# A four-layer gated cross-attention decoder: GpSimd's constants in pieces between its first stores, and two buffers of squares in the key preparation

## The reference, cut to what matters

```python
x = x + jnp.tanh(g_xattn[0]) * _L0_xattn_ref(_layernorm(x, axis=-1), ctx_1024, ctx_1024, L0_xattn_Wq, ...)
x = x + jnp.tanh(g_ffn[0]) * _L0_ffn_ref(_layernorm(x, axis=-1), ...)
...
x = x + jnp.tanh(g_xattn[2]) * _L2_xattn_ref(ctx_1024, _layernorm(x, axis=-1), L2_xattn_Wq, ...)
...
x = x + jnp.tanh(g_xattn[3]) * _L3_xattn_ref(ctx_1024, ctx_1024, _layernorm(x, axis=-1), mask_Bx1xS2_bf1, ...)
x = x + jnp.tanh(g_ffn[3]) * _L3_ffn_ref(_layernorm(x, axis=-1), ...)
```

```python
qh = (q @ Wq + bq).reshape(B, Lq, H, D).transpose(0, 2, 1, 3)
kh = (k @ Wk + bk).reshape(B, k.shape[1], H, D).transpose(0, 2, 1, 3)
vh = (v @ Wv + bv).reshape(B, v.shape[1], H, D).transpose(0, 2, 1, 3)
att = jnp.einsum('bhqd,bhkd->bhqk', qh, kh) * scale
att = jax.nn.softmax(att, axis=-1)
y = jnp.einsum('bhqk,bhkd->bhqd', att, vh)
```

## Time and profile before

| | |
|---|---|
| median of 3 runs | 3102.66 us (3099.45 to 3102.67) |
| the profiled execution's own time | 3106.83 us |
| its span in the profile | 3105.2 us |
| mean granted TensorE clock | 0.984 of full speed |
| busy: PE, ACT, DVE, POOL | 97%, 81%, 15%, 7% of the span |
| context preparation, first scores at | 118.06 us from the span's start |

### The profile page before, as it was taken

One profiled execution on the slowest core, in us unless ns is written; L12 is line 12 of the kernel. 1 busy time (PEld: TensorE's weight loads), 2 busy tenths in 40 slices (PEclk: granted clock), 3 DMA queues, 4 the chain that ended last, 5 costly groups with the idle time before them and its releaser, 6 DMA issues.

```text
span 3105.2 us, 54465 instructions
## 1 busy us (share of the span) xinstructions
PE 3003.0 (97%) x18636; PEld 1135.6 (37%) x18636; DVE 465.9 (15%) x1308; ACT 2520.9 (81%) x2893; POOL 205.7 (7%) x732
## 2 busy tenths in 40 slices
PE   5899999999999799999999998999899999999999
PEld 3333333323333433333333334666522222322257
DVE  2310010100011400111101004544200000100012
ACT  2699999999943399999999996322399999999963
POOL 3000000000000000000000002000000000000000
PEclk8999999999999899999999999999899999999999
DMA  5222122111230112122211124010011111111110
GB/s 156 74 65 72 49 68 72 37 37 57 62 86 1 25 56 63 55 68 65 65 38 39 58 61 120 30 38 1 5 38 37 37 37 50 51 38 37 37 38 7
DMA packets 167027, 157.25 MB, mean 51 GB/s; under 512 B 20872, under 2 KB 121724, under 8 KB 166844
## 3 DMA queue, kind: packets, MB, share of 16 engines
q1 hardware_dynamic: 159872, 149.27, 16.1%
q0 software_dynamic: 1088, 3.34, 0.3%
q10 hardware_dynamic: 5884, 2.08, 0.3%
HBM read 121.89 MB, written 32.91 MB: 50 GB/s over the span
## 4 chain that ended last, share of the span: by engine, by line
PE 93%; DVE 4%; issue 1%; ACT 1%; POOL 1%; DMA 0%; SPq 0%; ACTq 0%; DVEq 0%; POOLq 0%
PE PS L2299 40%; PE PS L2318 31%; PE PS L768 5%; PE PS L753 5%; PE PS L755 2%; PE PS L1108 2%; PE PS L1098 1%; PE PS L1566 1%; PE PS L1563 1%; PE PS L1142 0%; PE PS L1099 0%; PE PS L2279 0%; PE PS L2212 0%; PE PS L2285 0%; PE PS L1128 0%
## 5 line engine op out<-in xcount | busy, mean ns | idle before, releaser
L2074 ACT ACTIVATE probs<-PS 128x1024 f32<-128x1024 f32 x2496 | 2283.3, 1228 | 41.3 <-PE PS L2318 36.3
L2299 PE MATMUL PS<-probs,vr 128*32 128x512 f32 (+1 forms) x9984 | 1326.7, 604 | 1.9 <-DVE accs L2544 1.9
L2318 PE MATMUL PS<-qs,kr 35*128 35x512 f32 (+2 forms) x4992 | 1066.0, 482 | 8.1 <-issue 3.1
L2318 PEld LDWEIGHTS PS<-qs,kr 35*128 35x128 f32 x4992 | 448.8, 184 | 1183.3 <-ACT probs L2074 816.9
L791 ACT ACTIVATE probs<-PS 128x512 f32<-128x512 f32 x192 | 114.5, 598 | 272.8 <-PE PS L753 144.7
L1905 POOL COPY vr<-vs 128x72 f32 (+1 forms) x624 | 157.8, 253 | 2672.6 <-PE PS L2299 2474.5
L2299 PEld LDWEIGHTS PS<-probs,vr 128*32 128x32 f32 x9984 | 197.3, 108 | 339.7 <-issue 273.4
L768 PEld LDWEIGHTS PS<-wide,probs 128*128 128x128 f32 x1280 | 151.5, 194 | 17.5 <-issue 16.7
L768 PE MATMUL PS<-wide,probs 128*128 128x128 f32 x1280 | 153.8, 277 | 0.5 <-DVE kf L826 0.5
L2544 DVE COPY accs<-PS 128x512 f32<-128x512 f32 x12 | 8.3, 692 | 749.4 <-PE PS L2285 749.4
L753 PE MATMUL PS<-xT,wide 128*128 128x512 f32 x224 | 106.7, 594 | 1.0 <-DVE probs L810 1.0
(11 more groups left out here) (312 smaller groups left out, 1169.4 us busy)
## 6 DMA issues: line engine op xcount, KB each, us to landing
kr<-key_pieces SPq DMA_DIRECT2D x1248, 64.0 KB
key_pieces<-kparts SPq DMA_DIRECT2D x172, 96.0 KB, 2.8
kr<-mask_strips SPq DMA_DIRECT2D x624, 4.0 KB
values<-kf SPq DMA_DIRECT2D x34, 216.0 KB, 4.1
vs<-values SPq DMA_DIRECT2D x2, 3672.0 KB, 16.7
c_T<-turned_context SPq DMA_DIRECT2D x18, 192.0 KB, 4.0
key_pieces<-probs SPq DMA_DIRECT2D x32, 96.0 KB, 3.0
c_in<-turned_context SPq DMA_DIRECT2D x16, 192.0 KB, 4.1
```

The source lines that it names most:

```text
L2074: sc.activation(prob[n % RING][:, :, q0:], PS[:, bank:bank + 2, q0:], ACT.Exp, scale=SCALE).then_inc(p_ready, 1)
L2299: last = te.matmul(PS[32 * j:32 * j + 32, 7, q0:], vr[s.buf(c)][:, at_v:at_v + 32], prob[(n + j // 2) % RING][:, j % 2, q0:], start=fresh, ...
L2318: last = te.matmul(o, kr[b][own, p, :], qs[own, T8 // 2 * s.hh + p, 512 * s.qh + q0:512 * s.qh + 512], start=True, stop=True)
```

## The change

Three edits, all in the first 100 us of the program.

- **GpSimd's constants in pieces.** `const_ready` is signalled three times: behind `c_last`, which is now right behind `head_of`; behind a piece that holds what the mask and the last rows need; and behind the last constant. The other constants follow in pieces, each behind one of the first nine stores of `c_T`, whose loop is written out. ACT's wait behind step 0 is for the first signal. DVE's mask work comes behind step 2 and waits for the second. ACT (step 9), DVE (step 13) and PE (behind the preparation) wait for the third.
- **The chain with two buffers of squares.** The high part has a semaphore of its own, `k_high`; SP's first stores and DVE's low part wait for it. ACT's squares read the stored high part in SBUF instead of the keys in PSUM, into `ksq[:, b]`, and stand behind the copy of the next step. Their wait for the norms is one for two steps back, and so is PE's wait for the low part.
- **Small ones.** DVE's steps 3 to 12 are written out instead of looped. ACT issues the attention weights in steps 1 to 3 and the mask strips in step 4.

```diff
@@ gpsimd
             last.then_inc(first_const, 1)
-            g.memset(vs[:, :, :, HD:VC].rearrange("p c h o -> p (c h) o"), 1.0)
             g.memset(mask_u8[:, :], 0)
             chain(g.memset(c_last[:, :], 0.0))
-            g.memset(c_last[0:LAST, D:D + 1], 1.0)
-            pool.wait_ge(ident_ready, 1)
-            chain(g.tensor_copy(ident_b[:, :], ident[:, :]))
...
-            g.memset(run_max[:, :, :], 0.0).then_inc(const_ready, 1)
...
+            g.memset(c_last[0:LAST, D:D + 1], 1.0).then_inc(const_ready, 1)
+
+            def k_step(i):
+
+                pool.wait_ge(ct_ready, i + 1)
+                g.dma_start(ct_scr[i:i + 1, :, :].rearrange("o p k -> p (o k)"), c_T[i % 2]).then_inc(ct_out[i % 2], 16)
+
+            def row_constants():
+                g.memset(vs[:, :, :, HD:VC].rearrange("p c h o -> p (c h) o"), 1.0)
...
+            def mask_constants():
...
+                g.tensor_copy(ident_b[:, :], ident[:, :]).then_inc(const_ready, 1)
...
+            k_step(0)
+            row_constants()
+            k_step(1)
+            mask_constants()
+            k_step(2)
+            stair_constants()
+            k_step(3)
+            left_constants()
+            k_step(4)
+            pick_constants()
+            k_step(5)
+            chain(g.memset(leaf_sel[:, :, :], 0.0))
+            leaf_rows_pool(g, chain, (0,))
+            k_step(6)
+            leaf_rows_pool(g, chain, (1, 2))
+            k_step(7)
+            counts_pool(g, chain)
+            k_step(8)
+            mean_constants()
+            for i in range(9, NTILE):
+                k_step(i)
@@ sync
-                for c, done in enumerate((k_act, k_low)):
+                for c, done in enumerate((k_high, k_low)):
@@ scalar
-                if not first:
-                    act.wait_ge(kn_ps, at(j, off, 1, 0))
                 keys = PS[:, 1 + b, 0:TW]
-                sc.activation(kparts2[b][:, 0, :, 0, :], keys.rearrange("p (c k) -> p c k", c=TC), ACT.Identity, bias=bqk[:, 1, 0:1])
-                sc.activation(ksq[:, 0, :], keys, ACT.Square, bias=bqk[:, 1, 0:1]).then_inc(k_act, 1)
+                sc.activation(kparts2[b][:, 0, :, 0, :], keys.rearrange("p (c k) -> p c k", c=TC), ACT.Identity, bias=bqk[:, 1, 0:1]).then_inc(k_high, 1)
                 if not last:
                     rows(j, off + 1, first)
+                if not first:
+                    act.wait_ge(kn_ps, at(j, off, 1, -1))
+                act.wait_ge(k_high, at(j, off, 1, 1))
+                sc.activation(ksq[:, b, :].rearrange("p (c k) -> p c k", c=TC), kparts2[b][:, 0, :, 0, :].bitcast(F32), ACT.Square).then_inc(k_act, 1)
...
-                if i == 1:
+                if 1 <= i < 4:
+                    attention_weights(i - 1)
+                if i == 4:
                     strips()
-                if 2 <= i < 5:
-                    attention_weights(i - 2)
...
                 if i == 9:
+                    act.wait_ge(const_ready, 3)
                     router_weights(act)
@@ tensor
-                te.matmul(PS[0:32, 7, 0:TW], head_of[:, :], ksq[:, 0, :], start=True, stop=True).then_inc(kn_ps, 1)
+                te.matmul(PS[0:32, 7, 0:TW], head_of[:, :], ksq[:, off % 2, :], start=True, stop=True).then_inc(kn_ps, 1)
...
-                    pe.wait_ge(k_low, at(j, off, 1, 0))
+                    pe.wait_ge(k_low, at(j, off, 1, -1))
...
+            pe.wait_ge(const_ready, 3)
@@ vector
-                dve.wait_ge(k_act, at(j, off, 1, 1))
+                dve.wait_ge(k_high, at(j, off, 1, 1))
...
-            dve.wait_ge(const_ready, 1)
+            k_step(None, 1)
+            k_step(None, 2)
+            dve.wait_ge(const_ready, 2)
...
-            with dve.Fori(0, ROUNDS) as j:
-                for off in range(1, UNROLL + 1):
-                    k_step(j, off)
+            for i in range(3, TAIL[0]):
+                k_step(None, i)
             for k, i in enumerate(TAIL):
                 if k == 0:
                     dve.wait_ge(x_in, 16)
+                    dve.wait_ge(const_ready, 3)
```

More of the change, by code:

```diff
@@ L679, in flamingo_decoder, with leaf_rows_pool @@
         E1_IN = (16 * 9, 16 * 10)
-        def const_pool(g, chain):
-            chain(g.memset(leaf_sel[:, :, :], 0.0))
-            for n in range(3):
+        def leaf_rows_pool(g, chain, nets):
+            for n in nets:
                 ls = leaf_sel[:, :, :].rearrange("p c (l h) -> p c l h", l=2)
@@ L686, in const_pool, with counts_pool @@
                                       base=-32 * n, pattern=[[-2, HC], [-1, 2], [0, 64]], channel_multiplier=1))
+        def counts_pool(g, chain):
             chain(g.iota(countdown[:, :], pattern=[[-1, LEAVES]], base=LEAVES, channel_multiplier=0,
@@ L1840, in _ @@
             last.then_inc(first_const, 1)
-            g.memset(vs[:, :, :, HD:VC].rearrange("p c h o -> p (c h) o"), 1.0)
             g.memset(mask_u8[:, :], 0)
             chain(g.memset(c_last[:, :], 0.0))
-            g.memset(c_last[0:LAST, D:D + 1], 1.0)
-            pool.wait_ge(ident_ready, 1)
-            chain(g.tensor_copy(ident_b[:, :], ident[:, :]))
-            chain(g.memset(stair[:, :], 0.0))
-            chain(g.affine_select(out=stair[:, :], in_=stair[:, :], compare_op=ALU.is_ge, fill=-BIG,
-                                  base=0, pattern=[[1, P]], channel_multiplier=-1))
@@ L1850, in _ @@
[L1850 to L1878, removed]
@@ L1879, in _ @@
-            chain(g.affine_select(out=kvm, in_=kvm, compare_op=ALU.is_ge, fill=0.0,
-                                  base=HD - 1, pattern=[[HD, H], [0, HD]], channel_multiplier=-1))
-            g.memset(run_max[:, :, :], 0.0).then_inc(const_ready, 1)
[L1883 to L1888, removed]
@@ L1889, in _ @@
-            with pool.Fori(0, ROUNDS) as j:
-                for off in range(1, UNROLL + 1):
-                    k_step(j, off)
-            for i in TAIL:
-                k_step(None, i)
+            g.memset(c_last[0:LAST, D:D + 1], 1.0).then_inc(const_ready, 1)
[4 more added lines that the diff above has]
+                g.memset(vs[:, :, :, HD:VC].rearrange("p c h o -> p (c h) o"), 1.0)
+                g.memset(zero_one[:, 0, :], 0.0)
+                g.memset(zero_one[:, 1, :], 1.0)
+                chain(g.memset(valid[:, :], 1.0))
+                chain(g.affine_select(out=valid[:, :], in_=valid[:, :], compare_op=ALU.is_ge, fill=0.0,
+                                      base=CTX - 1, pattern=[[-1, P]], channel_multiplier=-P))
@@ new lines, in mask_constants, with stair_constants @@
+            def mask_constants():
+                g.memset(rows_w[:, :], 0.0)
+                g.memset(leaf_b2[:, :, :], 0.0)
+                g.memset(ones_row[:, :], 1.0)
+                chain(g.memset(valid_last[:, :], 0.0))
+                chain(g.memset(valid_last[0:LAST, :], 1.0))
+                pool.wait_ge(ident_ready, 1)
+                g.tensor_copy(ident_b[:, :], ident[:, :]).then_inc(const_ready, 1)
+            def stair_constants():
+                chain(g.memset(stair[:, :], 0.0))
+                chain(g.affine_select(out=stair[:, :], in_=stair[:, :], compare_op=ALU.is_ge, fill=-BIG,
+                                      base=0, pattern=[[1, P]], channel_multiplier=-1))
+                chain(g.memset(upper[:, :], 0.0))
+                chain(g.affine_select(out=upper[:, :], in_=upper[:, :], compare_op=ALU.is_ge, fill=-BIG,
+                                      base=0, pattern=[[-1, P]], channel_multiplier=1))
@@ new lines, in left_constants, with pick_constants @@
+            def left_constants():
+                for b in range(TC):
+                    g.memset(vr[b][:, :], 0.0)
+                g.memset(k_left[:, :].bitcast(F32), 0.0)
+                g.memset(v_left[:, :, :], 0.0)
+            def pick_constants():
+                g.memset(one_row[:, :], 0.0)
+                chain(g.memset(pick[:, :, :, :].bitcast(F32), 0.0))
+                for e in range(2):
+                    chain(g.memset(one_row[HALF * e + PROD:HALF * e + PROD + 1, :], 1.0))
+                for c in range(PARTS):
+                    for r in range(PARTS):
+                        at_r = PIECES * c + HD * r
+                        dst = pick[:, c].rearrange("p t (e x) -> p t e x", e=2)[:, :, :, at_r:at_r + HD]
+                        g.tensor_copy(dst, ident[:, :].rearrange("p (e d t) -> p t e d", e=2, d=HD))
@@ new lines, in mean_constants @@
+            def mean_constants():
+                chain(g.memset(kv_mask[:, :], 1.0))
+                kvm = kv_mask[:, :].rearrange("p (h d) -> p h d", h=H)
+                chain(g.affine_select(out=kvm, in_=kvm, compare_op=ALU.is_ge, fill=0.0,
+                                      base=0, pattern=[[-HD, H], [0, HD]], channel_multiplier=1))
+                chain(g.affine_select(out=kvm, in_=kvm, compare_op=ALU.is_ge, fill=0.0,
+                                      base=HD - 1, pattern=[[HD, H], [0, HD]], channel_multiplier=-1))
```

(1 more changed line is left out.)

5 lines of the change are left out of this document (1 added, 4 removed).

## The result

The changed kernel takes 3084.71 us (median of 5 runs, 3078.82 to 3087.39), the kernel before 3102.66 us (5 runs, 3099.45 to 3103.02). The ratio is 0.9942, 95% interval 0.9931 to 0.9954: faster by 18 us, 0.6%. The forecast was 3081 us, range 3072 to 3090. The profiled execution took 3084.71 us, its span is 3082.9 us, against 3106.83 and 3105.2 before.

What follows compares the result with a forecast made beforehand. Only the sweeps' start, 118.06 us in, could move, held by ACT's hole and a PE-DVE-ACT chain. 14.62 + 31.6 + 2.5 + 13.6 put keys(13) at 62.3, DVE's tail end at 78.5; gain 22 us: 3081 us, range 3072 to 3090.

Steps and rivals of the forecast that it cites:

- The hole goes: ACT's idle 14.0 us from 13.8 to 27.8 us, waiting for GpSimd's last constant, was to vanish with the early signal.
- Steps 1 to 8 at 3.95 us, bounded by SP, plus 2.5 us for one stall: SP's DMA issuing in its loop sets the pace, 31.6 us; one stall on stores of keys stays as before.
- Steps 9 to 12 at 3.4: SP's issues, written out from step 9 on, set 3.4 us a step, 13.6 us in all.
- The tail bounded by DVE, 15.5 us: Steps 13 to 16: DVE's own list, 13.6 us plus 1.9 us of semaphore gaps, ending at 78.5 us.
- From there on the same: From the end of DVE's tail to the first scores the program is unchanged.
- 22 us off the median: Gain of 22 us taken off the old kernel's median of 3102.66 us, giving 3081 us.
- Page against row: Skill page gives 435 GB/s for the DMA fabric; rows imply about 260 GB/s, so stores may land later than now.
- PE as the bound: Rival: steps 1 to 12 run at PE's 3.05 us each; gain 32.6 us, 3070 us; chance 0.12.
- The unchanged pace: Rival: the stores' landing replaces the chain, steps stay at 4.17 us; gain 16.7 us, 3086 us; chance 0.18.
- the slow case: Rival: TensorE's clock held at 0.50 through the loop, sweeps start some 8 us later; 3111 us; chance 0.03.
- Late stores by GpSimd: Rival: each of nine constant pieces makes ACT's copy a microsecond late; gain 13 us, 3090 us; chance 0.08.
- The signs: Marks named beforehand: ACT's longest wait, keys(13), SP's queue, first scores; steps over 4.1 us would refute it.

Runs made afterwards that it cites:

- experiment 2: Changed kernel with all of GpSimd's constants ahead of its first store, the three signals kept in place; 3097.57 us, ratio 0.9986 to the kernel before.
- The repeat: The changed kernel measured once more, word for word; 3084.34 us, ratio 0.9945 to the kernel before.
- experiment 4: Changed kernel with SP's loop over steps 1 to 8 written out; 3080.99 us, ratio 0.9932 to the kernel before.
- 12: Changed kernel with SP's loop written out, measured a second time, on the chip of the changed kernel's second measurement; 3082.02 us, ratio 0.9937 to the kernel before.
- Experiment 9: Changed kernel with a second GpSimd DMA of 192 KB a step to a scratch tensor; 3087.96 us, ratio 0.9959 to the kernel before.
- experiment 8: Changed kernel with one wait put back, PE's keys(i) waiting for low(i-1) again; 3091.27 us, ratio 0.9961 to the kernel before.
- experiment 10: Changed kernel with two more DMAs of 0.5 KB a step on SP's queue; 3091.53 us, ratio 0.9968 to the kernel before.
- experiment 1: Changed kernel with the chain's edits undone, constants still in pieces; 3094.14 us, ratio 0.9974 to the kernel before.
- 3: Changed kernel with all constants ahead of the first store, ACT's and DVE's first waits for the last constant; 3096.18 us, ratio 0.9980 to the kernel before.

## Why the prediction was right, point by point

- *The hole goes*: right. The stores between the pieces are needed (experiment 2); that the early signal is needed too follows from ACT's wait of 14.0 us for it before, and no run has the stores early and the signal late.
- *Keys(1) at 14.62*: 15.09. Off by half a microsecond; PE's Gram products of step 0 ran until then. The repeat had 14.29.
- *Steps 1 to 8 at 3.95 us, bounded by SP, plus 2.5 us for one stall*: 34.1 us forecast, 47.22 - 15.09 = 32.1 measured. The sum held, its terms did not. The long steps 5 and 6 took 11.3 us, 3.4 more than two steps of 3.95, and the other six took 3.5 on average, down to 2.9. SP's queue was full on average, as forecast, but the steps are not even: ACT waits for landings, then catches up from the two buffers. In the repeat the same eight steps took 36.1 us, so that the forecast lies between the two is partly luck. The bound itself is a little off in the working: 3.78 and at least 0.2 are 3.98, not 3.95.
- *Steps 9 to 12 at 3.4*: 63.88 - 47.22 = 16.7 us, 4.2 each. This term failed by 3 us, by 1.1 in the repeat (14.7), by 0.7 and 1.2 in experiments 4 and 12. SP's own pauses are 0.5 us there. The high parts of steps 9, 11 and 12 waited 3.70, 2.60 and 2.17 us for stores, and that of step 10 stood behind seven small DMAs of the router's weights, a list of ACT's that the forecast left out. As in experiment 4, a shorter issue on SP does not give 3.4: the landing takes over.
- *The tail bounded by DVE, 15.5 us*: DVE's last maximum ends at 79.09 us, forecast 78.5, and DVE is busy 13.82 of the last 15.24 us. Right, and 3.3 us shorter than before (18.51).
- *From there on the same*: 95.70 - 79.09 = 16.6 us against 118.06 - 100.04 = 18.0. Before, PE waited 3.13 us for "issue" ahead of the first scores; now 0.89. The repeat, the same kernel, waited 2.10 there, so this is the execution's and not a gain of the change: luck, of up to 2.2 us.
- *22 us on the profile's scale*: 22.1. *22 us off the median*: 18.0, and 17.1 in the repeat. This is the step that was mis-sized. "The median of the three runs is 4.2 us lower" was taken off both kernels alike; but the profiled execution of before lay at the upper end of its own spread (3097.50 to 3106.89 in 23 later runs), while that of the changed kernel lay on its median. A part of the 22.4 us was luck of the two executions: against the repeat's profile it is 19.9.
- *Page against row.* The trace: DMA share 0.87 at 252 GB/s in the hole's old place, 0.77 at 216 in step 6, 0.75 at 181 in the tail (first fence above), so, as an estimate from these rows, 240 to 290 GB/s at full share for these transfers. By the Trainium skill, "DMA: Bandwidth & Descriptors", section Bandwidth, the fabric would carry 435 GB/s. The trace does not reach it. That stores land later than before is small or absent: 3.0 and 3.1 us at a share of 0.78 (20 to 62 us), 3.2 and 3.4 at 0.75 in the repeat, 3.0 and 3.2 at 0.75 before (27 to 81 us). Experiment 9, with a share of 0.84, has 3.8 and 4.0.
- *The rivals.* PE as the bound appears in single steps (2.8 us) but not in the sum. The unchanged pace is what experiment 8 gives. The clock fell behind the long step (0.62 in step 6; 0.51 in step 7 of the repeat) and was 1.00 in the hole's old place: the slow case is out. Late stores by GpSimd: the store of step 3 left at 22.34 us, straight behind its copy; none is among the longest waits. DVE and GpSimd do get in each other's way, as that rival feared, but it is DVE that waits (last section).
- *The signs.* Keys(13) between 59 and 66 us, first scores near 96, a queue of SP with hardly a gap, nothing moved behind: these held. ACT's longest wait before 100 us was to be under 5 us and was 5.5, 7.4 in the repeat, and several steps of the loop took over 4.1 us, which by the forecast's own words would make it wrong; but it had also put one stall of 2.5 us into its sum, and such a stall cannot be without a step over 4.1. That sign was set badly.

**What stays open** is how the strips, 220 KB in three DMAs, stretch the issues and landings behind them: the DMA engines are not full then, their share in the long step is 0.61, the lowest of the rows shown. Waits of up to 4.7 us, one of 5.1 in step 2 of the repeat and one of 5.8 in experiment 10 come without the strips. No kernel was clearly better than the changed one; the version with SP's loop written out was 2 to 4 us faster in both of its runs, within the intervals.

## What to carry to other kernels

A setup list on a little-used engine costs nothing until that engine also has a store that a buffer waits for: put the setup behind the stores, piece by piece, and count both the signal and the store as ways for the list to hold others up. When a chain of turn-taking engines is opened, add up first each issuing queue's time per step, DMA issues with the register work between them, since that queue is the next bound, and then ask what is right behind it: here a relief of 0.5 us a step in the queue brought almost nothing. A gain read between two single profiles carries the luck of both; the medians decide. A small transfer that is moved takes the wait behind it along: look at the issues next to it, at its old place and at its new one.

## What the runs showed of the hardware

The one thing not expected is on DVE. A `tensor_scalar` of 64 x 128 in SBUF takes 0.21 us where no memset of GpSimd falls beside it (experiments 1, 2, 3 and 9), and 2.70 us in the changed kernel, 2.69 in its repeat and in experiment 10, where GpSimd starts its memsets just behind it. In experiment 8 the cast ahead of it (0.21 us in the changed kernel) was held instead, for 1.71 us, to just behind the end of the memsets, and the `tensor_scalar` took 0.21. Timelines of DVE and GpSimd in the changed kernel:

```profile
22.29 0.22 DVE L2430 TENSOR_SCALAR mask_fill<-valid 64x128 f32<-64x128 f32 x1
22.43 2.70 DVE L2431 TENSOR_SCALAR mask_fill<-mask_f 64x128 f32<-64x128 f32 x1
```

```profile
22.90 0.87 POOL L1878 MEMSET vr<- 128x272 f32 x3
23.69 1.10 POOL L1879 MEMSET k_left<- 128x1184 f32 x1
24.72 0.33 POOL L1880 MEMSET v_left<- 128x256 f32 x1
```

It ends at 25.13 us, just behind the last memset of the piece (25.05), and the memsets kept their lengths (experiment 1, without overlap, has the same). The Trainium skill, "SBUF — State Buffer", section SBUF: two separate sides, has VectorE and GpSimd lock a shared pair of ports against each other, the one that starts first keeping it for its instruction. The trace agrees that one waits for the other; but by the recorded starts DVE's operation was first and still waited, and for five memsets. In the changed kernel no cost shows. In experiment 4 it does: the cast took 2.65 us and the `tensor_scalar` 2.38, DVE's low part of step 3 ended only at 27.97 us, and SP's queue stood still for it for 1.3 us.
